# Dividing the product for a query head: six matmuls among a unit's tiles, six at its end

## What is computed

```
xn  = layernorm(x)
q   = rope(xn @ Wq.T)                      # 32 heads of 128
k,v = low-rank keys and values, 8 heads
p   = softmax(causal(q @ k.T / sqrt(128)))
out = x + (p @ v) @ Wo.T + ffn(xn)
```

## Time and profile before

| what | before |
|---|---|
| median of 3 runs | 2416.55 us |
| the profiled execution | 2418.7 us |
| its span in the profile | 2416.8 us |
| PE busy | 2341.2 us, 97% |
| DVE, ACT, POOL busy | 61%, 47%, 39% |
| mean granted TensorE clock | 0.993 |

### The profile page before, as it was taken

The page is one execution under the profiler, slowest core; times in us unless marked ns, Lnnn a source line. Parts: engine busy times, 40 slices in busy tenths (PEclk is TensorE's granted clock), DMA queues, the critical chain, the costliest instruction groups (busy, mean ns, idle before and its releaser), DMA issues.

```text
span 2416.8 us, 35041 instructions
## 1 busy us (share of the span) xinstructions
PE 2341.2 (97%) x11840; PEld 1972.8 (82%) x11840; DVE 1477.3 (61%) x3641; ACT 1133.3 (47%) x2217; POOL 939.3 (39%) x813
## 2 busy tenths in 40 slices
PE   6999999999899999999999999999999999999998
PEld 5777877777788888888888888888888888888877
DVE  5343343424676766666676767666766667666765
ACT  3452524335454544445444545454544445454544
POOL 1000000000554554545454545455454545454543
PEclk9999999999999999999999999999999999999999
DMA  5676757789412121221212152312212131303110
GB/s 194 187 283 189 254 176 227 263 264 335 157 44 106 44 97 62 88 98 43 105 44 105 36 191 82 129 44 96 78 72 105 36 114 36 112 29 114 35 53 18
DMA packets 103810, 286.56 MB, mean 119 GB/s; under 512 B 9072, under 2 KB 42352, under 8 KB 92528
## 3 DMA queue, kind: packets, MB, share of 16 engines
q1 hardware_dynamic: 101552, 280.53, 34.1%
q10 hardware_dynamic: 2112, 4.19, 0.5%
HBM read 200.80 MB, written 83.89 MB: 118 GB/s over the span
## 4 chain that ended last, share of the span: by engine, by line
PE 70%; DVE 3%; issue 2%; ACT 2%; DMA 1%; POOL 1%; SPq 1%; POOLq 0%; ACTq 0%; DVEq 0%
PE ob L1093 16%; PE scores L1067 15%; PE qb L1048 14%; PE ob L1108 13%; PE ptb L1079 10%; DVE pT L1009 1%; DMA ff_raw<-in_ffw 1%; PE ring L844 1%; PE ring L829 1%; SPq L556 1%; ACT long_prob L951 1%; ACT pT L966 1%; PE down L853 0%; DVE q_sin L1004 0%; DVE q_sin L1003 0%
## 5 line engine op out<-in xcount | busy, mean ns | idle before, releaser
L966 ACT ACTIVATE pT<-ptb 128x512 fp32r<-128x512 f32 x576 | 335.5, 594 | 506.7 <-PE ptb L1079 504.1
L1093 PE MATMUL ob<-pT,v_sb 128*128 128x512 f32 x1728 | 476.3, 405 | 7.0 <-DVE pT L1009 7.0
L1009 DVE TENSOR_TENSOR pT<-ptb,pT 128x512 fp32r<-128x512 f32 x576 | 390.8, 688 | 96.0 <-ACT pT L966 92.3
L937 POOL TENSOR_TENSOR q_cos<-q_cos,q_sin 128x512 f32<-128x512 f32 x125 | 161.9, 1295 | 559.8 <-DVE q_cos L1005 559.8
L931 POOL TENSOR_TENSOR long_prob<-long_prob,rinv 128x384 f32<-128x384 f32 (+3 forms) x256 | 304.7, 1203 | 171.4 <-DVE rinv L1027 171.4
L1048 PE MATMUL qb<-xT,wq 128*128 128x512 f32 x1488 | 358.2, 390 | 0.0
L1093 PEld LDWEIGHTS ob<-pT,v_sb 128*128 128x128 f32 x1728 | 304.2, 188 | 59.5 <-DVE pT L1009 13.7
L931 POOL TENSOR_TENSOR short_prob<-short_prob,rinv 128x512 f32<-128x512 f32 (+3 forms) x256 | 278.4, 1095 | 189.0 <-DVE rinv L1027 186.2
L1067 PE MATMUL scores<-kT,late_qT 128*128 128x384 f32 (+3 forms) x1536 | 343.9, 359 | 0.0
L1048 PEld LDWEIGHTS qb<-xT,wq 128*128 128x128 f32 x1488 | 279.3, 188 | 59.5
L1067 PEld LDWEIGHTS scores<-kT,late_qT 128*128 128x128 f32 x1536 | 264.3, 188 | 27.5 <-POOL late_qT L941 4.0
(11 more groups left out here) (95 smaller groups left out, 2994.4 us busy)
## 6 DMA issues: line engine op xcount, KB each, us to landing
wq<-w_parts SPq DMA_DIRECT2D x126, 512.0 KB, 3.6
w_parts<-stage SPq DMA_DIRECT2D x32, 1024.0 KB, 4.9
ff_raw<-in_ffw SPq DMA_DIRECT2D x56, 384.0 KB, 3.8
k_parts<-stage SPq DMA_DIRECT2D x128, 128.0 KB, 2.3
v_parts<-stage SPq DMA_DIRECT2D x64, 256.0 KB, 3.6
w_raw<-in_wqo SPq DMA_DIRECT2D x32, 512.0 KB, 5.7
kT<-k_parts SPq DMA_DIRECT2D x16, 1024.0 KB, 7.4
v_sb<-v_parts SPq DMA_DIRECT2D x16, 1024.0 KB, 8.8
```

The costliest lines, as they stand in the source:

```text
L937: nc.gpsimd.tensor_tensor(qc, qc, qs, ALU.add).then_inc(q_turned, 1)
L966: nc.scalar.activation(pT[:, t % 4, HI], ptb[t % 2][:], ACT.Copy).then_inc(pT_hi, 1)
L1009: nc.vector.tensor_tensor(pT[:, t % 4, LO], ptb[t % 2][:], pT[:, t % 4, HI].bitcast(F32), ALU.subtract).then_inc(pT_split, 1)
L1093: mm = nc.tensor.matmul(ob[:], v_sb[e % 2][:, x, j], pT[:, t % 4, y], start=(j == 0 and (x, y) == (HI, HI)), stop=(is_last(kind, n, j) and ...
```

## The change

Q is split into "QF", the products of the first half of the contraction (six matmuls), and "Q", those of the second half (six). QF stands at place 0.5 of a step, ahead of S3 (0.7); Q stays at the end, at 1.0. The waits of the product move to QF; `q_done` is still raised by the last matmul of Q. The planner takes 1.36 for each half. In the opening the two halves stand next to each other.

```diff
-PLACES = (("S", 0, 0.0), ("W", 0, 0.15), ("S", 1, 0.2), ("S", 2, 0.3), ("S", 3, 0.7), ("Q", 0, 1.0))
+PLACES = (("S", 0, 0.0), ("W", 0, 0.15), ("S", 1, 0.2), ("S", 2, 0.3), ("QF", 0, 0.5), ("S", 3, 0.7), ("Q", 0, 1.0))
-OPENING = [("Q", 0, 0), ("Q", 1, 0), ("Q", 2, 0), ("S", 0, 0), ("Q", 3, 0), ("S", 0, 1), ("Q", 4, 0),
-           ("S", 0, 2), ("Q", 5, 0), ("S", 0, 3)]
+OPENING = [("QF", 0, 0), ("Q", 0, 0), ("QF", 1, 0), ("Q", 1, 0), ("QF", 2, 0), ("Q", 2, 0), ("S", 0, 0),
+           ("QF", 3, 0), ("Q", 3, 0), ("S", 0, 1), ("QF", 4, 0), ("Q", 4, 0), ("S", 0, 2), ("QF", 5, 0),
+           ("Q", 5, 0), ("S", 0, 3)]
...
-            n = k + {"S": 0, "Q": AHEAD, "W": -2}[kind]
-            if kind == "Q" and k < EARLY:
+            n = k + {"S": 0, "QF": AHEAD, "Q": AHEAD, "W": -2}[kind]
+            if kind in ("QF", "Q") and k < EARLY:
...
 def product_needs(kind, n, j, tiles):
+    if kind == "QF":
+        return [("dve", "Q", n - 1, 0)] if n >= AHEAD else []
     if kind == "Q":
-        return [("dve", "Q", n - 1, 0)] if n >= AHEAD else []
+        return []
...
-    return {"Q": 2.72, "T": 0.44, "PV": 0.72, "W": 2.72}[kind]
+    return {"QF": 1.36, "Q": 1.36, "T": 0.44, "PV": 0.72, "W": 2.72}[kind]
...
-                if kind == "Q":
+                if kind in ("QF", "Q"):
                     x = n // AHEAD % 2
...
+                    if kind == "QF":
+                        (the waits for x_ready, the weights and q_read, as before)
                     bank = query_bank(n)
-                    for k in range(KC):
+                    for k in range(0, KC // 2) if kind == "QF" else range(KC // 2, KC):
...
-                    mm.then_inc(q_done, 1)
+                    if kind == "Q":
+                        mm.then_inc(q_done, 1)
```

More of the change, by code:

```diff
@@ L1032, in heads_tensor @@
                 e, i = unit_kv(n), unit_block(n)
-                if kind == "Q":
+                if kind in ("QF", "Q"):
                     x = n // AHEAD % 2
[L1035 to L1044, removed]
+                    w_q = opening_wq[:, n - 2] if n in (2, 3) else wq[:, n % 2]
+                    if kind == "QF":
+                        if n % BATCH in (0, AHEAD):
+                            pe.wait_ge(x_ready[x], (n // BATCH + 1) * 16)
+                        if n in (2, 3):
+                            pe.wait_ge(opening_loaded, 64)
+                        else:
+                            pe.wait_ge(wq_loaded[n % 2], n // 2 * 16 + 16)
+                        if n >= AHEAD:
+                            pe.wait_ge(q_read, n if n >= AHEAD + EARLY else n - AHEAD + 1)
                     bank = query_bank(n)
-                    for k in range(KC):
+                    for k in range(0, KC // 2) if kind == "QF" else range(KC // 2, KC):
                         for m, (w, p) in enumerate(PASSES):
```

## The result

The changed kernel takes 2488.86 us (median of 4 runs, 2488.23 to 2490.58), against 2418.07 us for the kernel before (4 runs, 2415.39 to 2420.49; the three of the forecast and one more). The ratio is 1.0294, 95% interval 1.0276 to 1.0312: slower by 2.9%, where 2491 us was forecast. The profiled execution has a span of 2488.7 us, 71.9 more than before.

A forecast was written before the change was run, and what follows sets the result against it. PE was taken to bound the kernel, busy 97% of the span. 15 x (3.4 stall + 1.7 clock) = 76.5, plus 7.4, less 9, gave 75 us over the 2416.55 us median: 2491 us, range 2455 to 2520 us.

The forecast's parts named there:

- The order of DVE and POOL: Step 4 into 5: Q ahead of INV on DVE and of NORM on POOL; T0 3.4 us late, 15 times.
- Rivals 3 and 4: Rival 3, and a faster case: INV ahead of Q, EXP of S3 ahead of oT on ACT; 2404 us, chance 0.06.
- rival 3: Step 4 into 5: INV is not behind Q, T0 only 0.35 us late; 2420 us, chance 0.08.
- The clock: Half clock behind each of 15 stalls at T0 of step 5 costs 1.7 us; bounds nothing and 3.4 us.
- rival 2: Step 4 into 5: longer stall or second stretch of half clock, 15 x 1.7 us more; 2517 us, chance 0.12.
- Rival 1: Stall where step 4 meets step 5, without the clock's price: 2466 us, chance 0.12.
- the mean clock: Sign in the changed kernel's timeline: granted clock dips once a period and its mean falls to about 0.97.
- Where step 7 meets step 0: T0 waits for NORM of S3's head, 0.49 us late in 15 periods: 7.4 us lost.
- Gain: Waits won by QF's earlier place: about 9 us from B in step 3; C counted inside step 4's sum.
- B: Step 3: the last PV follows its T too closely; the wait goes, about 9 us over 16 periods.
- C: Step 4: S3 waits 0.34 us for QL; QF covers it, counted inside the sum for step 4.
- A: Step 1: a transpose waits for DVE; the wait stays, as QF falls behind T3.

The follow-up runs named there:

- the first experiment: Changed kernel's divided PE list, with DVE, ACT and POOL keeping the orders of the kernel before: 2420.14 us, ratio 0.9991 against the kernel before.
- the filled stall: Changed kernel with thirteen useless matmuls ahead of T0 in step 5, inside the stall: 2467.64 us, ratio 1.0197 against the kernel before.
- the second experiment: Undivided PE list of the kernel before, with DVE, ACT and POOL taking the changed kernel's orders: 2509.3 us, ratio 1.0361 against the kernel before.

## Why the prediction was right

Forecast was 2491 us, measured 2488.86. The nearness of the two is in part luck: the forecast stood on 2416.55 us and added 75, and what came is 70.8 above a median of 2418.07 (72.0 between the traces).

*The order of DVE and POOL.* This was the step that carried the forecast, and it held to the item: both swaps are in the trace, and the two crossed experiments show that the orders are the cause. Dividing everywhere but in step 4 leaves the other differences of the orders in place and has no stall, so it is the change of the orders at this one boundary. T0 was forecast 3.4 us late and came 3.44 late. Rivals 3 and 4 fall with it; rival 3 is what the first experiment measures when the order is held: T0 starts 1.82 us behind S0 where 1.22 would do, 0.60 late, and the rival had 1565.05 - 1564.36 = 0.69.

*The clock.* Forecast at 1.7 us a stall. In the window from T0 to T1 above it is 4.75 x (1 - 0.66) = 1.6, and the same stretch took 1567.89 - 1564.70 = 3.19 us before, 1.56 less. Its end in the kernel before:

```profile
1567.89 0.60 PE L1079 MATMUL ptb<-ident,short_prob 128*128 128x128 f32 x4
```

Two of the fifteen stalls, though, were followed by a stretch of half clock about twice as long, as rival 2 has it. Ten microseconds around T0, first in one of those two periods, then in the common case, and in each T0 and T2:

```profile
1139.00:1149.00 10.00, 9.38 (x36) 7.85 (x37) 3.59 (x8) 2.88 (x7) 3.46 (x3) 0.66 0.01 2
1606.00:1616.00 10.00, 9.25 (x44) 7.99 (x45) 4.78 (x10) 4.20 (x9) 3.59 (x3) 0.83 0.00 0
```

```profile
1139.62 1.11 PE L1083 MATMUL ptb<-ident,short_prob 128*128 128x128 f32 x4 [3.53 <-POOL short_prob L934]
...
1147.36 0.60 PE L1083 MATMUL ptb<-ident,short_prob 128*128 128x128 f32 x4
```

```profile
1606.75 1.11 PE L1083 MATMUL ptb<-ident,short_prob 128*128 128x128 f32 x4 [3.53 <-POOL short_prob L934]
...
1613.16 0.60 PE L1083 MATMUL ptb<-ident,short_prob 128*128 128x128 f32 x4
```

From T0 to T2 it is 7.74 us and 6.41, so the long stretch costs 1.3 us more. Fifteen dips at 1.6 and twice 1.3 make 26.6 us, where 25.5 was forecast and the filled stall measured 21 to 24. Rival 1, a stall without the clock, is excluded by the filled stall.

The price itself was taken from one stall, the 2.82 us of the earlier trace rows. An idle of the same length at the same place has no price in the trace of the second experiment: from T0 to T1 it is 2443.05 - 2439.79 = 3.26 us there, against 2352.30 - 2347.47 = 4.83 in the kernel before (its T1 first, then the second experiment).

```profile
2352.30 0.60 PE L1079 MATMUL ptb<-ident,short_prob 128*128 128x128 f32 x4
```

```profile
2439.79 0.66 PE L1088 MATMUL ptb<-ident,short_prob 128*128 128x128 f32 x4 [2.82 <-POOL short_prob L939]
...
2443.05 0.60 PE L1088 MATMUL ptb<-ident,short_prob 128*128 128x128 f32 x4
```

That a dip would follow each of the fifteen longer stalls, as it did, was more than one row could tell.

Of the signs named, one was off by its own arithmetic: the mean clock was to fall to about 0.97 and fell to 0.981. Fifteen times 1.7 us are 1% of the span, which takes 0.993 to 0.983.

*Where step 7 meets step 0.* Forecast 0.49 us; T0 starts 1543.04 - 1542.20 = 0.84 behind the start of S0, whose three matmuls take 0.68 (1503.72 - 1503.04 before): 0.16 us. The wait is too short for the list of PE's waits, where 0.5 us of `long_prob` had been named as a sign. I had moved the whole chain behind S3 by 1.36 us. But before the change the maximum of that head came late on DVE, behind a tile of T. First the changed kernel, then the kernel before (S3 on PE, its maximum on DVE):

```profile
1536.63 1.63 PE L1071 MATMUL scores<-kT,late_qT 128*128 128x512 f32 x6
...
1538.31 1.22 DVE L991 CUSTOM_DVE_ANT_0 long_prob<-scores,mask 128x1024 f32<-128x1024 f32 x1
```

```profile
1607.89 1.64 PE L1067 MATMUL scores<-kT,late_qT 128*128 128x512 f32 x6
...
1609.29 0.69 DVE L1009 TENSOR_TENSOR pT<-ptb,pT 128x512 fp32r<-128x512 f32 x1 [0.32 <-ACT pT L966]
1609.90 1.22 DVE L988 CUSTOM_DVE_ANT_0 long_prob<-scores,mask 128x1024 f32<-128x1024 f32 x1
```

From start to start it is 1.68 us now and was 2.01: 0.33 of the 0.49 comes back, which leaves the 0.16. The sum was mis-sized by 5 us in this term.

*Gain.* B was taken at 9 us. Step 3 alone gave 10 us in the medians and 0.69 us a period. In the period shown step 3 lasts 9.06 us (1582.65 to 1591.71) against 9.71 (1543.39 to 1553.10). C and A went as forecast, one away and one not.

*The sum.* In the period shown: 3.44 + 1.6 + 0.16 - 0.65 for B is 4.55, against 4.59 measured (116.37 - 111.78). Fifteen times 4.59 and two longer dips at 1.3 more make 71.5, against 72.0 between the two windows. The forecast said 75. The term where step 7 meets step 0 takes 5 off it and B another 0.8; the longer dips give back about 1 and T0's 0.04 a period 0.6. These terms leave about 1 us unexplained.

The Trainium skill (TensorE: Matmul & The Clock Gate, "What's actually happening") says that the phase of the clock gate does not follow the kernel. The two stalls of 2.38 us with different ends agree with that; no run here shows the phase itself.

## What to carry to other kernels

A list scheduler that never holds an engine back can put a long, unimportant item ahead of a short, urgent one that is ready a moment later; moving a product on one engine can flip such a pair on another, and the flip can cost far more than the move (here 3.6% by the orders alone, nothing that can be told by the moved products alone). So after any move, compare the orders of all engines item by item, and test the list and the orders crosswise. Divide filler work where a wait is to be covered (here steps 1 and 3, 0.8% together) and leave it whole where it covers the chain to the next step.

## What was unexpected of the hardware

An idle of 2.38 us on PE was followed by half clock at 901 us and not at 787 us, in one execution, with the same work around. After 3.53 us it was followed by half clock in all thirty stalls of the changed kernel and of the second experiment, for twice as long in nine of them. Useless matmuls in a stall paid: 195 of them took 21 to 24 us off the kernel, since the clock stayed at 0.994 in the mean instead of 0.981.
